# A GNN kernel's edge stages: units evicted one slot later, attribute loads moved from ScalarE to SyncE, twelve cell buffers

## What is computed

```python
h = relu(layernorm(x))
for l in range(2):                                   # layers 0 and 1 of the kernel
    msg = relu(h[src] + edge_attr)                   # one row of 128 per edge
    agg = segment_sum(msg, dst)
    h = mlp_with_batchnorm(h + agg)                  # W1[l], gamma, beta, W2[l]
x = x + h
h = relu(layernorm(x))
for l in range(2):                                   # layers 2 and 3 of the kernel
    h = mlp((1 + eps[l]) * h + segment_sum(h[src], dst))
x = x + h
```

## Time and profile before

| | |
|---|---|
| plain runs, median of 3 (lowest to highest) | 2762.56 us (2761.05 to 2769.45) |
| profiled execution, span from first to last instruction (no time beside it is shown) | 3625.8 us |
| PE busy | 2077.8 us (57%) |
| DVE busy | 1694.3 us (47%) |
| POOL busy | 1941.4 us (54%) |
| ACT busy | 734.2 us (20%) |
| mean granted TensorE clock | 0.755 of full speed |

### The profile page before, as it was taken

The page is one execution under the profiler, slowest core; times in us unless marked ns, Lnnn a source line. Parts: engine busy times, 40 slices in busy tenths (PEclk is TensorE's granted clock), DMA queues, the critical chain, the costliest instruction groups (busy, mean ns, idle before and its releaser), DMA issues.

```text
span 3625.8 us, 35066 instructions
## 1 busy us (share of the span) xinstructions
PE 2077.8 (57%) x9399; PEld 1269.9 (35%) x9399; DVE 1694.3 (47%) x2880; ACT 734.2 (20%) x1002; POOL 1941.4 (54%) x2048
## 2 busy tenths in 40 slices
PE   2454545545555552454545554535568778778888
PEld 1332323323332332232323232323334444444445
DVE  5655556555555553465646564545652122312112
ACT  3121212212122241222222222223340000300001
POOL 5655656555655526565655565556234555265552
PEclk7676667766767776777777777776778888888889
DMA  5232322323233332333333333334324444344442
GB/s 153 79 98 82 94 90 91 97 83 102 89 102 93 101 98 67 105 102 106 104 103 112 111 110 112 114 107 131 107 90 160 131 156 139 95 153 158 135 133 83
DMA packets 228544, 396.82 MB, mean 109 GB/s; under 512 B 43080, under 2 KB 133020, under 8 KB 228388
## 3 DMA queue, kind: packets, MB, share of 16 engines
q0 software_dynamic: 65024, 133.30, 14.3%
q1 hardware_dynamic: 111684, 162.15, 12.8%
q10 hardware_dynamic: 51680, 99.63, 7.8%
HBM read 333.10 MB, written 61.81 MB: 109 GB/s over the span
## 4 chain that ended last, share of the span: by engine, by line
another core or an unknown queue 29%; PE 24%; issue 21%; DVE 12%; ACT 9%; DVEq 3%; ACTq 2%; POOL 0%; DMA 0%; SPq 0%
PE psA L1536 13%; PE psG L1551 5%; ACT xp_room L785 3%; ACT psG L758 3%; DVE cell_room L1116 3%; DVE xp_room L1130 2%; DVEq L1051 2%; DVE hid L1076 2%; PE psA L1493 1%; PE psG L1509 1%; DVE xp_room L1095 1%; ACT count_out L741 1%; ACTq L751 1%; PE psG L1600 1%
## 5 line engine op out<-in xcount | busy, mean ns | idle before, releaser
L674 POOL DMA_INDIRECT xg<-node_table,src_all x1520 | 1438.1, 946 | 1087.4 <-DVE xp_room L1130 566.7
L1493 PE MATMUL psA<-cell_room,xp_room 128*128 128x512 f16 (+1 forms) x2336 | 712.5, 450 | 967.5 <-ACT count_out L741 609.5
L694 POOL DMA_INDIRECT xg<-node_table,idx x480 | 467.9, 975 | 519.9 <-issue 358.4
L1493 PEld LDWEIGHTS psA<-cell_room,xp_room 128*128 128x128 f16 x2336 | 258.7, 114 | 1384.3 <-ACT count_out L741 658.2
L1130 DVE TENSOR_TENSOR xp_room<-psG,xg 128x512 f32<-128x512 f32 x380 | 255.3, 672 | 938.8 <-ACT psG L758 910.9
L1116 DVE TENSOR_SCALAR cell_room<-psG,cell_all 128x932 f16<-128x932 int16 x1088 | 683.8, 683 | 16.7 <-remote 16.7
L1509 PE MATMUL psG<-hid,xp_room 128*128 128x160 f32 x3072 | 522.2, 336 | 265.3 <-DVE hid L1076 208.2
L1509 PEld LDWEIGHTS psG<-hid,xp_room 128*128 128x128 f32 x3072 | 504.4, 221 | 304.5 <-issue 302.0
L758 ACT COPY psG<-xp_room 128x512 f32<-128x512 f32 x384 | 226.7, 590 | 1486.0 <-issue 692.8
L1029 DVE TENSOR_TENSOR acc<-acc,row_slot 128x38 f32 x192 | 38.3, 200 | 636.9 <-ACT row_slot L837 529.3
L1536 PE MATMUL psA<-cell_room,xp_room 128*128 128x456 f16 x1200 | 274.8, 383 | 98.1 <-issue 76.1
(11 more groups left out here) (156 smaller groups left out, 817.4 us busy)
## 6 DMA issues: line engine op xcount, KB each, us to landing
xp_room<-in_edge_attr_dram ACTq DMA_DIRECT2D x95, 768.0 KB
cell_room<-count_store SPq DMA_DIRECT2D x16, 2850.0 KB
count_store<-count_out SPq DMA_DIRECT2D x96, 465.5 KB
hid<-count_store SPq DMA_DIRECT2D x16, 2736.0 KB
xg<-node_table,src_all POOLq DMA_INDIRECT x1520
xp_room<-in_edge_attr_dram ACTq DMA_DIRECT2D x95, 256.0 KB
row_slot<-node_table SPq DMA_DIRECT2D x1024, 0.5 KB
hid<-node_table SPq DMA_DIRECT2D x1024, 0.5 KB
```

What stands on the lines that cost most here:

```text
L674: nc.gpsimd.indirect_dma_start(xg[:, n % 2, u, j, :], None, x if n < RAW_TURNS else table, bass.IndirectOffsetOnAxis(ap=src_all[:, s, j:j ...
L694: nc.gpsimd.indirect_dma_start(xg[:, q, u, j, :], None, table, bass.IndirectOffsetOnAxis(ap=idx[:, q, u, j:j + 1], axis=0),).then_inc(row_ ...
L1493: last = nc.tensor.matmul(psA[:, bank, 0:w], src_hot[:, hots(n) % 2, at, :], cells[:, c % CELL_RING, c0:c0 + w], start=first, stop=end)
```

## The change

SyncE issues the attribute loads: `load_ahead(n + 1)` stands at the head of its turn n and waits for `scattered` of turn n - 2. Its row loads follow, and the stores of units stand last. ScalarE's `load_behind` is deleted. Units are evicted at a gate: at the earliest one slot behind their last chunk, at least two slots behind the unit before, and within the layer's counting turns. TensorE places each piece at its chunk's slot or at the slot behind the gate of the unit before it, whichever is later, so that pieces can slip behind the window products of their turn. The cell ring has twelve buffers, the six new ones in the room of `rows_h`; the one-hot rows have three. VectorE waits for the node table to be written before it first writes into `rows_h`. No line of GpSimd's program is edited.

```diff
-CELL_RING = 6
+CELL_RING = 12
+ROOM_CELLS = 6
+HOT_RING = 3
...
+def unit_gates():
+
+    gates, last = [], -1
+    for k in range(UNITS):
+        built = SLOT_OF[(UNIT_END[k] - 1) // 2]
+        stop = (built // SLOTS // TURNS + 1) * TURNS * SLOTS - SLOTS - 1
+        last = min(max(built + 1, last + 2), stop)
+        gates.append(last)
+    return gates
...
+def piece_step(c, p0):
+
+    k = UNIT_OF[2 * c + p0 // HALF]
+    return max(SLOT_OF[c], UNIT_GATE[k - 1] + 1) if k > 0 else SLOT_OF[c]
...
+            def load_ahead(n):
+
+                if not RING <= n < EDGE_TURNS:
+                    return
+                used = n - RING
+                sp.wait_ge(scattered[used % 2], sp.snap(rounds * (used // 2 + 1) + 1))
+                load_turn(n)
+
             def edges(layer):
                 for n in range(layer * TURNS, (layer + 1) * TURNS):
-                    for k in units_in(turn_chunks(n)):
-                        sp.wait_ge(count_evicted, k + 1)
-                        sp.dma_start(count_store[k], count_out[:, k % 2, :]).then_inc(count_stored[k % 2], 16)
+                    load_ahead(n + 1)
                     gather_rows(layer, n % TURNS)
+                    for u in range(SLOTS):
+                        for k in units_at(n * SLOTS + u):
+                            sp.wait_ge(count_evicted, k + 1)
+                            sp.dma_start(count_store[k], count_out[:, k % 2, :]).then_inc(count_stored[k % 2], 16)
...
-            def load_behind(n):
-
-                if n < 0 or n + RING >= EDGE_TURNS:
-                    return
-                act.wait_ge(scattered[n % 2], act.snap(rounds * (n // 2 + 1) + 1))
-                t, slots, last = attributes_of(n + RING)
-                act.dma_start(ea[:, t, 0:SLOTS - 1, :, :].rearrange("p u j d -> p u (j d)"), slots).then_inc(ea_loaded[t], 16)
-                act.dma_start(ea[:, t, SLOTS - 1, :, :].rearrange("p j d -> p (j d)"), last).then_inc(ea_loaded[t], 16)
...
                             if u == slots[-1]:
                                 messages(n, slots)
-                            if u == (SLOTS - 1 if n == RAW_TURNS else 1):
-                                load_behind(n - 1)
-                            units_out(slot_chunks(n, u))
+                            units_out(i)
...
+                if n % TURNS == RAW_TURNS:
+                    dve.wait_ge(table_written, 16 * LG * (n // TURNS + 1))
+                if hots(n) > HOT_RING:
+                    dve.wait_ge(cells_used, USED_AFTER[turn_chunks(COUNTING[hots(n) - 1 - HOT_RING])[-1]])
...
-                    build_counts(n)
+                    for u in range(SLOTS):
+                        build_counts(n * SLOTS + u)
                     edge_windows(layer, n)
```

More of the change, by code:

```diff
@@ L122, in slot_chunks @@
     return [c for i, c in enumerate(chunks) if 1 + i * (SLOTS - 1) // len(chunks) == u]
-def units_in(chunks):
-    return [UNIT_OF[e] for c in chunks for e in (2 * c, 2 * c + 1) if e + 1 in UNIT_END]
 def row_work(t):
@@ L172, in parted, with units_at @@
     return [c for c in chunks if len(PIECES[c]) > 1]
+COUNTING = [n for n in range(EDGE_TURNS) if turn_chunks(n)]
+TURN_OF = {c: n for n in COUNTING for c in turn_chunks(n)}
+SLOT_OF = {c: n * SLOTS + u for n in COUNTING for u in range(SLOTS) for c in slot_chunks(n, u)}
 def hots(n):
-    return sum(len(turn_chunks(t)) > 0 for t in range(n + 1))
+    return COUNTING.index(n) + 1
+def unit_gates():
[6 more added lines that the diff above has]
+    return gates
+UNIT_GATE = unit_gates()
+def piece_step(c, p0):
+    k = UNIT_OF[2 * c + p0 // HALF]
+    return max(SLOT_OF[c], UNIT_GATE[k - 1] + 1) if k > 0 else SLOT_OF[c]
+STEPS = {}
+for c in range(CHUNKS):
+    for p0, p1 in PIECES[c]:
+        STEPS.setdefault(piece_step(c, p0), []).append((c, p0, p1))
+def units_at(i):
+    return [k for k, g in enumerate(UNIT_GATE) if g == i]
 MOST_CHUNKS = max(len(turn_chunks(n)) for n in range(EDGE_TURNS))
@@ L187 @@
 LAYERS = 4
-assert TURNS % 2 == 1 and 2 * SLOTS * EPP * WIN <= CELL_RING * CB
+assert TURNS % 2 == 1 and 2 * SLOTS * EPP * WIN <= ROOM_CELLS * CB
 assert SUPERS % SLOTS == 0 and OVERLAP % EPP == 0 and SECOND <= P
@@ L192 @@
 assert CB % 2 == 0 and CB - IOTA <= IOTA <= 1024 and MOST_CHUNKS <= CELL_RING and EPP * D == 512
-assert CBANKS == 4 and UPG * CW <= 512 and HALF_B * UPG >= CELL_RING * BLOCKS // 2
+assert CBANKS == 4 and UPG * CW <= 512 and HALF_B * UPG >= ROOM_CELLS * BLOCKS // 2
 def group_blocks(g):
@@ L315, in gnn_kernel @@
             "p (q c w) -> p q c w", q=2, w=WIN)
-        cell_room = sb("cell_room", [P, max(UPG * HALF_B * CW, CELL_RING * CB)], F16)
+        cell_room = sb("cell_room", [P, max(UPG * HALF_B * CW, ROOM_CELLS * CB)], F16)
         last_hot = cell_room[:, 0:2 * SLOTS * EPP * WIN].bitcast(F32).rearrange("p (u j w) -> p u j w", u=SLOTS, j=EPP)
-        cells = cell_room[:, 0:CELL_RING * CB].rearrange("p (r c) -> p r c", c=CB)
+        room_cells = cell_room[:, 0:ROOM_CELLS * CB].rearrange("p (r c) -> p r c", c=CB)
+        more_cells = rows_h[:, :, :].rearrange("p b d -> p (b d)").bitcast(F16)[
+            :, 0:(CELL_RING - ROOM_CELLS) * CB].rearrange("p (r c) -> p r c", c=CB)
+        cells = [room_cells[:, i, :] for i in range(ROOM_CELLS)] + [
+            more_cells[:, i, :] for i in range(CELL_RING - ROOM_CELLS)]
         counts = [cell_room[:, 0:UPG * HALF_B * CW].rearrange("p (s c) -> p s c", s=UPG),
@@ L332, in gnn_kernel @@
         w_rows = xp_room[:, 0:8 * D].bitcast(F32).rearrange("p (k d) -> p k d", d=D)
[L334 to L336 removed]
+        src_hot = xp_room[:, 8 * D:(8 + HOT_RING * MOST_HOTS) * D].bitcast(F16).rearrange(
+            "p (h j d) -> p h j d", h=HOT_RING, d=D)
+        LN0 = (8 + HOT_RING * MOST_HOTS) * D
         ln_stats = xp_room[:, LN0:LN0 + 12 * BLOCKS].bitcast(F32).rearrange("p (b k) -> p b k", k=6)
@@ L733, in centre_raw, with units_out @@
                     last.then_inc(raw_centred, 1)
-            def units_out(chunks):
-                for k in units_in(chunks):
+            def units_out(i):
+                for k in units_at(i):
                     act.wait_ge(cells_used, UNIT_USED[k])
@@ L1087, in chunk_rows @@
                     return
[L1088 to L1092, removed]
+                slot = hots(n) % HOT_RING
+                if n % TURNS == RAW_TURNS:
+                    dve.wait_ge(table_written, 16 * LG * (n // TURNS + 1))
+                if hots(n) > HOT_RING:
+                    dve.wait_ge(cells_used, USED_AFTER[turn_chunks(COUNTING[hots(n) - 1 - HOT_RING])[-1]])
                 def rows_hot(at, c0, c1):
@@ L1115, in chunk_cells @@
                 for c0, c1 in CELL_PARTS:
-                    nc.vector.tensor_scalar(cells[:, c % CELL_RING, c0:c1], iota_bank[:, 0:c1 - c0],
+                    nc.vector.tensor_scalar(cells[c % CELL_RING][:, c0:c1], iota_bank[:, 0:c1 - c0],
                                             float(c0), cell_all[:, c:c + 1], ALU.add, ALU.is_equal
@@ L1474, in turn_rows, with build_counts @@
                     last.then_inc(cols_turned, 1)
[L1476 to L1480, removed]
-                        pe.wait_ge(src_hot_ready, hots(n))
[L1482 to L1495, removed]
+            def build_counts(i):
+                for c, p0, p1 in STEPS.get(i, ()):
+                    n = TURN_OF[c]
+                    chunks = turn_chunks(n)
+                    if c == chunks[0] and p0 == 0:
+                        pe.wait_ge(src_hot_ready, hots(n))
+                    k = UNIT_OF[2 * c + p0 // HALF]
+                    first = 2 * c + p0 // HALF == UNIT_END[k] - UNIT_SIZES[k]
+                    end = 2 * c + p1 // HALF == UNIT_END[k]
+                    if first and k > 0:
+                        pe.wait_ge(count_evicted, k)
+                    pe.wait_ge(cells_ready, 2 * (c + 1))
+                    at = len(chunks) + parted(chunks).index(c) if p0 else c - chunks[0]
+                    for bank in range(CBANKS):
+                        c0 = bank * 512
+                        w = min(512, CB - c0)
+                        last = nc.tensor.matmul(psA[:, bank, 0:w], src_hot[:, hots(n) % HOT_RING, at, :],
+                                                cells[c % CELL_RING][:, c0:c0 + w], start=first, stop=end)
+                    last.then_inc(cells_used, 1)
             def edge_windows(layer, n):
```

1 line of the change is left out of this document (removed).

## The result

The changed kernel takes 2774.54 us (median of 4 runs, 2773.91 to 2775.44), the kernel before 2761.81 us on the same chip (4 runs, 2760.59 to 2769.45). The ratio is 1.0043, 95% interval 1.0031 to 1.0056: slower by 12.7 us, which is more than the 8 us that the prediction took as what a run can tell. Forecast were 2718 us and a chance of 0.18 for slower.

What follows compares the result with a forecast made beforehand. The prediction took waits as the bound, first VectorE's for ScalarE's copies behind attribute loads and evictions. It summed 2762.6 - 49 (later evictions) + 5 (layer 1's last turn) = 2718 us, other parts 0, range 2615 to 2800.

Steps and rivals of the forecast that it cites:

- Carrying it over: Step from stretched trace to plain runs: plain edge turns of 16.3 to 17.9 us, a plain gather at most 1.02 to 1.12.
- the slack of 0.7 to 2.3 us a turn: Plain edge turn above VectorE's own 15.6 us; 67 to 218 us in all, owed to ScalarE's waits or GpSimd.
- Evicted later: 29 units ending in slot 1, evicted a slot later, free the last slot's copy: 1.7 us each, -49 us.
- no loss now, none after: Units ending in slots 2 and 3: evicted behind copies needed six microseconds later, so the change costs nothing there.
- Layer 1's last turn: VectorE waits for all cells while three delayed pieces stand behind the windows: 0 to 12 us, 5 taken.
- Loads on SyncE: SyncE issues the attribute load, then 24 row loads and count stores: 11.9 us a turn, hidden, value 0.
- SyncE as the bound: Rival: count stores behind row loads delay ScalarE's copy once a row costs over 0.45 us; 2830 us, chance 0.18.
- Cells, one-hot slots, `table_written`: Twelve cell buffers, three one-hot slots and VectorE's new table wait: value 0, bounds -17 to 0.
- Late semaphores (second rival): `scattered` some 3 us late in plain runs too, so all slack goes: -142 us, 2620 us, chance 0.14.
- The first rival: GpSimd's gathers already fill the plain edge turn, so no change: 2755 to 2770, say 2762 us, chance 0.28.

Runs made afterwards that it cites:

- E0: The kernel before, unchanged, profiled once more: 2761.81 us, profiled span 2760.0 us.
- E10: The kernel before with half of GpSimd's gathers left out (slots 1 and 3 from the third turn of a layer on): 2327.29 us, ratio 0.8432.
- E11: The changed kernel with the same half of GpSimd's gathers left out: 2312.65 us, ratio to before 0.8377.
- E2: The kernel before with only the attribute loads moved to SyncE, a turn ahead: 2759.58 us, ratio 0.9992.
- E1: The changed kernel, but no piece put off past the last counting turn of its layer: 2765.37 us, ratio to before 1.0013.
- E3: The kernel before with a quarter of the gathers of layers 0 and 1 left out (slot 3 from the third turn on): 2332.39 us, ratio 0.8445.
- E8: The same kernel as E3, run again for its timeline: 2332.93 us, ratio 0.8453.

## Why the prediction was wrong

**The step that failed** is in "Carrying it over": "the plain turn is shorter, so a plain gather costs at most 1.02 to 1.12 us". It rests on the sentence before: each late pair takes 57.3 us with TensorE busy 45.98, "so at best 14 x 11 = 154 us go". Both floors were read from a stretched execution, and busy time was taken as something that cannot shrink. It can: the chain of waits in layer 2 of E0, to be read beside the earlier trace rows:

```profile
2117.98 14.72 PE psA L1536 x75
2132.70 4.35 PE psG L1551 x32
2137.04 14.52 PE psA L1536 x72
2151.56 4.35 PE psG L1551 x32
2155.91 14.72 PE psA L1536 x75
```

A pair takes 2155.91 - 2117.98 = 37.93 us, not 46 to 57: 14 pairs give back 271 us, not 154. The products of the counts (L1493) last 378 ns in E0 and 450 in the earlier trace rows. Taken between the same sums of VectorE as in the earlier trace rows, the edge turns of E0 last 873.0 us (122.45 to 995.41) and 962.4 us (1046.30 to 2008.73), 19.3 us each where 16.3 to 17.9 were worked out; all else is 2760.0 - 1835.4 = 924.6 us, 293 less than in the stretched execution, not 154. The turn by GpSimd's stride, 16 x 1.25 = 20.0 us, which the prediction had from the earlier trace rows, needed no reduction. Everything behind it fell with it: the slack of 0.7 to 2.3 us a turn above VectorE's 15.6 belongs to GpSimd, and is some 4.4 us.

- **Evicted later, -49 us (0 to -81):** nothing in the full kernel, where VectorE waits 377.9 us for gathered rows (E0) and what it needs sooner meets rows that aren't there. The mechanism itself was right: with GpSimd out of the way the 29 turns hold 40.1 us of waits behind the late copy (E10), 1.4 each where 1.7 were taken. But "no loss now, none after", said of units that end in slots 2 and 3, is wrong: eight gates fall in slot 1, where the eviction delays the copy again, 29.7 us (E11).
- **Layer 1's last turn, +5 us (0 to 12):** right mechanism, at its upper end. VectorE's wait is 11.86 us and the stretch to layer 2 is 13.5 us longer. The reason for choosing 5, that the last gathers are late anyway, was wrong: after the change VectorE waits there for TensorE, and the sums of rows come behind that wait.
- **Loads on SyncE, 0:** nearly right (E2: 0.9983 to 1.0001). A small gain in the trace was missed, the pauses of 4.15 and 4.36 us at the beginning of layer 0. E2 keeps 5.5 of the 8.5 us in its gathers and the stretch behind them. The loads are 95, not 92, which makes the upper bound 89 us in place of 86. On the Trainium skill, "DMA: Bandwidth & Descriptors", "Issuing engines are not separate DMA queues", only issue time is saved by another issuer: the trace agrees, with 0.94 us a turn freed on an engine that waits 1224.0 us for VectorE (E0's L758), and no time that can be told.
- **SyncE as the bound:** decided from 0.45 us a row by the prediction; measured are 8.96 us for 24 rows in E0, 0.37 us each, beside 0.96 in the earlier trace rows.
- **Cells, one-hot slots, `table_written`:** not tried by themselves. E1, which holds all three, is within 4 us of before.
- **Late semaphores (second rival):** the 11 us between TensorE's rows and its semaphore were those of the stretched execution. In E0 the window matmuls of a turn end at 402.00 us by the profile, and ScalarE issues the load that waits for them at 402.04.

The first rival, GpSimd as the bound (0.28, 2762 us), was right about the turn. Its time missed the end of layer 1: 2762 + 12 is the result. Its gather of 1.02 to 1.12 us was the failed step's, too short. What spoke for it stood in the text: 20.0 us of gathers a turn. What was held against it, GpSimd's wait of 566.7 us in the earlier trace rows, was a wait of that one execution.

## What to carry to other kernels

When the profiled execution is far longer than the plain runs, have another one before a sum is made; if there is none, ask of every row whether it could be stretched, busy times too, and trust first a stride that has no wait in it and is the same all over the trace. Then add up for each engine what its own stride alone needs (here 16 x 1.25 us a turn): an engine whose sum fills the plain time is the bound, whatever share the chain gives it. A pause that the profile puts down to "issue" can still belong to a wait: set the turns that have it beside those that have not, and look what came late. And an order that is harmless in 95 turns can cost all it has in the last one, where nothing is left to hide it.

## What the runs showed of the hardware

- One and the same kernel had profiled spans of 3625.8 and 2760.0 us. In the long one TensorE's semaphores came some 11 us after the recorded ends, its matmuls lasted 450 ns in place of 378, and SyncE's row loads 0.96 us in place of 0.37; GpSimd's gathers kept 0.94 and 0.30 us. What causes it is open. The first profile of the cut kernel, E3's, was stretched as well, to 3742.9 us beside E8's 2327.6, but otherwise: its count products lasted 636 ns (E8: 375) at a granted clock of 1.000, while 24 row loads took 8.56 us, as quick as in E0.
- Where GpSimd waits for nothing, a gather of 128 rows of 512 bytes starts 1.25 us after the one before it in all these runs, whether VectorE is busy for 72% or 95% of the stretch.
- VectorE's add of windows, whose place in `acc` is read at run time, starts at least 1.98 us after the end of the copy that released the sum before it, in 92 turns of E10; the profile shows what is left of this behind the sum as "issue".
